# An expert stage on one core: two row tiles to a turn, half-height down matmuls, silus later, rows turned earlier, gathers in other chunks

## What is computed

```python
xn = _layernorm(x, axis=-1)
s = _L0_attn_ref(xn, w_qkv, w_out)
g = _silu(_L0_ffn_ref(xn, gate_w, wg, wu, wd))
x = x + s * g
```

```python
expert_idx = jnp.argmax(logits, axis=-1)
g = jnp.einsum('th,ehd->etd', xf, wg)
u = jnp.einsum('th,ehd->etd', xf, wu)
inter = jnp.square(jax.nn.relu(g)) * u
out = jnp.einsum('etd,edh->th', inter * onehot.T[:, :, None], wd)
```

## Time and profile before

| | |
|---|---|
| median of 3 runs | 1468.5 us (1468.19, 1468.5, 1473.36) |
| the profiled execution | 1476.87 us |
| its span, first to last instruction | 1475.1 us |
| mean granted share of the TensorE clock | 0.995 |
| PE, DVE, ACT, POOL busy | 1447.4, 1342.1, 1193.1, 161.7 us |

### The profile page before, as it was taken

How to read it: one execution, slowest core, us unless ns; L and a number is a source line. 1 busy time by engine, 2 the same in 40 slices (tenths; PEclk the granted TensorE clock), 3 DMA queues, 4 the chain that set the end, 5 groups by cost and what they waited for, 6 DMA issues and landing times.

```text
span 1475.1 us, 32004 instructions
## 1 busy us (share of the span) xinstructions
PE 1447.4 (98%) x11201; PEld 650.2 (44%) x11201; DVE 1342.1 (91%) x1979; ACT 1193.1 (81%) x2381; POOL 161.7 (11%) x221
## 2 busy tenths in 40 slices
PE   7999999999999999999999999999999999999988
PEld 5655444443485443444444444444444444444326
DVE  6689999999846998999999999999999999999806
ACT  3653488889867997898888898888898988998990
POOL 5333322200001221000000000000010000000110
PEclk9999999999999998999999999999999999999999
DMA  5875244426254455323233353332323523333323
GB/s 181 275 203 149 60 85 84 77 46 120 44 180 101 80 109 101 48 45 46 40 48 47 47 104 48 48 48 44 45 46 47 101 44 46 48 48 48 70 70 118
DMA packets 79801, 119.55 MB, mean 81 GB/s; under 512 B 28962, under 2 KB 66210, under 8 KB 72738
## 3 DMA queue, kind: packets, MB, share of 16 engines
q1 hardware_dynamic: 73714, 105.82, 36.2%
q0 software_dynamic: 3072, 8.39, 2.4%
q10 hardware_dynamic: 2896, 3.62, 0.7%
HBM read 77.15 MB, written 39.71 MB: 79 GB/s over the span
## 4 chain that ended last, share of the span: by engine, by line
PE 86%; DMA 8%; ACT 2%; issue 2%; DVE 1%; SPq 0%; POOL 0%; POOLq 0%; ACTq 0%
PE ps L1244 35%; PE ps L1258 33%; DMA gate<-ys_d,arena 7%; PE ps L1232 5%; PE ps L1160 3%; ACT arena L659 2%; PE ps L1438 2%; PE ps L1161 1%; PE ps L1391 1%; PE ps L1375 1%; PE ps L1193 1%; PE ps L1185 1%; PE ps L1172 1%; PE ps L1342 1%; PE ps L1137 0%
## 5 line engine op out<-in xcount | busy, mean ns | idle before, releaser
L1232 PE MATMUL ps<-ks,qs 48*128 48x512 f32 x1984 | 689.1, 443 | 0.0
L1244 PE MATMUL ps<-qs,ks 50*128 50x512 f32 x2048 | 679.2, 435 | 0.5 <-ACT arena L663 0.3
L810 DVE TENSOR_REDUCE arena<-ps 128x1 f32<-128x512 f32 x992 | 635.7, 676 | 12.4 <-PE ps L1232 12.2
L659 ACT ACTIVATE arena<-ps 128x512 f32<-128x512 f32 x1056 | 566.8, 606 | 78.8 <-PE ps L1244 67.0
L813 DVE TENSOR_REDUCE arena<-ps 128x1 f32<-128x1024 f32 x496 | 601.1, 1212 | 2.3 <-PE ps L1232 2.2
L659 ACT ACTIVATE x_sb<-ps 128x512 f32<-128x512 f32 x992 | 535.4, 598 | 64.1 <-PE ps L1244 47.9
L1244 PEld LDWEIGHTS ps<-qs,ks 50*128 50x128 f32 x2048 | 327.7, 185 | 475.6 <-issue 179.9
L1232 PEld LDWEIGHTS ps<-ks,qs 48*128 48x128 f32 x1984 | 325.0, 184 | 11.2 <-issue 3.0
L1258 PE MATMUL ps<-arena 128*32 128x256 f32 (+1 forms) x3104 | 308.6, 469 | 9.3 <-ACT arena L659 4.1
L1258 PE MATMUL ps<-x_sb,arena 128*32 128x256 f32 (+1 forms) x2960 | 291.1, 465 | 0.0
L1258 PEld LDWEIGHTS ps<-arena 128*32 128x32 f32 x3104 | 62.4, 108 | 129.1 <-issue 125.3
(11 more groups left out here) (116 smaller groups left out, 623.6 us busy)
## 6 DMA issues: line engine op xcount, KB each, us to landing
qs<-parts_d SPq DMA_DIRECT2D x186, 128.0 KB
ks<-parts_d SPq DMA_DIRECT2D x186, 128.0 KB
parts_d<-arena SPq DMA_DIRECT2D x64, 256.0 KB, 2.8
xs_d<-arena SPq DMA_DIRECT2D x13, 384.0 KB, 3.6
arena<-xs_d SPq DMA_DIRECT2D x13, 384.0 KB, 4.0
ys_d<-arena SPq DMA_DIRECT2D x13, 384.0 KB, 2.8
x_sb<-in_x SPq DMA_DIRECT2D x2, 2048.0 KB, 13.2
onum_d<-arena SPq DMA_DIRECT2D x124, 32.0 KB
```

The lines of the kernel that those rows point to most:

```text
L659: nc.scalar.activation(prob_of(pi, s, kb)[:, c * W:(c + 1) * W], ps[:, bank, :], ACT.Exp, scale=SCALE).then_inc(exp_done[bank], 1)
L810: nc.vector.tensor_reduce(most[head_slot][:, tile, u:u + 1], ps[:, AB + lo, :], AX.X, ALU.max).then_inc(a_reduced[u], 1)
L1232: ins = nc.tensor.matmul(ps[:, AB + c, :], qs[head_slot][ABASE:ABASE + KR, tile * P:(tile + 1) * P].bitcast(F32R), ks[head_slot][ABASE:ABA ...
L1244: nc.tensor.matmul(ps[:, bank, :], ks[s][at:at + KS, kb * P:(kb + 1) * P].bitcast(F32R), qs[s][at:at + KS, c * W:(c + 1) * W].bitcast(F32R ...
```

## The change

Two tiles, 2j and 2j+1, share a step j of PE, ACT and DVE. Each tile's hidden rows fill half of a 128-column `inter`, so one transpose serves both, and one tile's hidden rows come out on partitions 0 to 63, the other's on 64 to 127. The down weights are loaded twice, to both partition halves; each down matmul contracts 64 rows. For odd tiles POOL first copies the expert's lower-half weights to one of two buffers (`stage_down`), for even ones PE reads them by register. Rows are turned two tiles ahead, into banks 0 and 5 in turn, and `xsT` has four buffers. ACT takes the silus of tiles 2j-6 and 2j-5 at the head of its step j. `hr`, `hu` and the new weight buffers take the place of `turn`, which is no longer needed then. POOL's two memsets for zeroed halves go. SC is 11.

```diff
-    TB, EB, YB = 0, 1, 6
+    TBS, EB, YB = (0, 5), 1, 6
+    XB = 4
     XR = 3
-    SC = 14
+    SC = 11
...
-                for i in range(2):
-                    sp.dma_start(wd2[0:DE, :, :].rearrange("p (c i) d -> p c i d", i=2)[:, :, i, :],
-                                 wd_in[i * DE:(i + 1) * DE, :, :]).then_inc(expert_weights, 16)
+                for half in range(2):
+                    for i in range(2):
+                        rows = wd2[half * DE:(half + 1) * DE, :, :].rearrange("p (c i) d -> p c i d", i=2)
+                        sp.dma_start(rows[:, :, i, :], wd_in[i * DE:(i + 1) * DE, :, :]).then_inc(expert_weights, 16)
 
...
                 act.wait_ge(xs_turned, i + 1)
-                if i >= 2:
-                    act.wait_ge(hid_done, i - 1)
-                nc.scalar.copy(xsT[i % 2], ps[:, TB, 0:D].rearrange("p (k t) -> p k t", k=KC)).then_inc(xs_out, 1)
+                if i >= XB:
+                    act.wait_ge(hid_done, i - XB + 1)
+                nc.scalar.copy(xsT[i % XB], ps[:, TBS[i % 2], 0:D].rearrange("p (k t) -> p k t", k=KC)).then_inc(xs_out, 1)
 
...
-                for i in range(NF + 2):
-                    if i + 1 < NF:
-                        turned_out(i + 1)
-                    if i < NF:
-                        act.wait_ge(hid_done, i + 1)
-                        if i >= 2:
-                            act.wait_ge(inter_ready, i - 1)
-                        nc.scalar.activation(hr[i % 2], ps[:, EB + i % 2, 0:DE], ACT.Relu).then_inc(relu_done, 1)
-                    if i >= 2:
-                        act.wait_ge(y_done, i - 1)
-                        g, z = divmod(i - 2, FG)
-                        if g >= XR and z == 0:
-                            act.wait_ge(y_stored[g % XR], g // XR * 16)
-                        nc.scalar.activation(ysb[g % XR][:, z, :], ps[:, YB + i % 2, 0:D], ACT.Silu).then_inc(y_out, 1)
+                turned_out(1)
+                for j in range(NF2 + 3):
+                    for i in (2 * j - 6, 2 * j - 5):
+                        if 0 <= i < NF:
+                            act.wait_ge(y_done, i + 1)
+                            g, z = divmod(i, FG)
+                            if g >= XR and z == 0:
+                                act.wait_ge(y_stored[g % XR], g // XR * 16)
+                            nc.scalar.activation(ysb[g % XR][:, z, :], ps[:, YB + i % 2, 0:D], ACT.Silu).then_inc(y_out, 1)
+                    for i in (2 * j, 2 * j + 1):
+                        if i + 2 < NF:
+                            turned_out(i + 2)
+                        if i < NF:
+                            act.wait_ge(hid_done, i + 1)
+                            if i >= 2:
+                                act.wait_ge(inter_ready, i - 1)
+                            nc.scalar.activation(hr[i % 2], ps[:, EB + i % 2, 0:DE], ACT.Relu).then_inc(relu_done, 1)
 
...
-                for i in range(NF + 1):
-                    if i < NF:
+                for j in range(NF2 + 1):
+                    for i in (2 * j, 2 * j + 1):
+                        if i >= NF:
+                            continue
                         dve.wait_ge(relu_done, i + 1)
                         nc.vector.tensor_tensor(hu[i % 2], hr[i % 2], ps[:, EB + i % 2, DE:2 * DE], ALU.mult).then_inc(hu_ready, 1)
                         dve.wait_ge(hu_ready, i + 1)
-                        if i == 0:
-                            dve.wait_ge(pads_zeroed, 3)
-                        if i >= 2:
-                            dve.wait_ge(inter_turned, i - 1)
-                        nc.vector.tensor_tensor(inter[i % 2][:, 0:DE], hu[i % 2], hr[i % 2],
+                        if j >= 2:
+                            dve.wait_ge(inter_turned, j - 1)
+                        nc.vector.tensor_tensor(inter[j % 2][:, i % 2 * DE:(i % 2 + 1) * DE], hu[i % 2], hr[i % 2],
                                                 ALU.mult).then_inc(inter_ready, 1)
-                    if i >= 1:
-                        dve.wait_ge(inter_turned, i)
-                        if i >= 3:
-                            dve.wait_ge(y_done, i - 2)
-                        nc.vector.tensor_copy(interT[(i - 1) % 2], ps[:, PVB, 0:P]).then_inc(inter_out, 1)
+                    if j >= 1:
+                        dve.wait_ge(inter_turned, j)
+                        if j >= 3:
+                            dve.wait_ge(y_done, 2 * (j - 2))
+                        nc.vector.tensor_copy(interT[(j - 1) % 2], ps[:, PVB, 0:P]).then_inc(inter_out, 1)
 
...
+            def stage_down():
+
+                pool.wait_ge(expert_ready, 1)
+                pool.wait_ge(expert_weights, 16 * 8)
+                pool.wait_ge(v_staged[1], FB + 1)
+                for i in range(1, NF, 2):
+                    g, z = divmod(i, FP)
+                    if z == 1:
+                        packed = pool.value_load(expert[0:1, g:g + 1], min_val=0, max_val=E ** FP - 1)
+                    which = pool.snap(packed // E ** z % E, min_val=0, max_val=E - 1)
+                    if i >= 4:
+                        pool.wait_ge(y_done, i - 3)
+                    if i > 1:
+                        pool.wait_ge(down_staged, i // 2)
+                    nc.gpsimd.tensor_copy(down_up[i // 2 % 2][DE:P, :].unsqueeze(1),
+                                          wd2[DE:P, bass.ds(which, 1), :]).then_inc(down_staged, 1)
+
...
-            nc.gpsimd.memset(wd2[DE:P, :, :], 0.0).then_inc(pads_zeroed, 1)
-            pool.wait_ge(pads_zeroed, 2)
-            for i in range(2):
-                ins = nc.gpsimd.memset(inter[i][:, DE:P], 0.0)
-            ins.then_inc(pads_zeroed, 1)
-            pool.wait_ge(pads_zeroed, 3)
             for pi in range(2, FB):
                 for s in range(2):
                     stage(0, pi, s, pi)
             for s in range(2):
                 stage(0, FB, s, FB)
+            stage_down()
             collect(0, SC)
...
-                if i:
-                    pe.wait_ge(xs_out, i)
+                if i >= 2:
+                    pe.wait_ge(xs_out, i - 1)
                 for k in range(KC):
-                    last = nc.tensor.transpose(ps[:, TB, k * P:(k + 1) * P], xs[g % XR][:, z, k * P:(k + 1) * P], ident[:])
+                    last = nc.tensor.transpose(ps[:, TBS[i % 2], k * P:(k + 1) * P], xs[g % XR][:, z, k * P:(k + 1) * P], ident[:])
                 last.then_inc(xs_turned, 1)
 
...
             def experts():
...
+                pe.wait_ge(a_reduced[GROUP_OF[TBS[1] - AB]], past(FB * 2 * KB + AHEAD - KB))
+                turn_sorted(1)
+                pe.wait_ge(expert_weights, 16 * 8)
+                for j in range(NF2 + 2):
+                    for i in (2 * j, 2 * j + 1):
+                        if i + 2 < NF:
+                            turn_sorted(i + 2)
+                        if i < NF:
+                            pe.wait_ge(xs_out, i + 1)
+                            if i >= 2:
+                                pe.wait_ge(relu_done, i - 1)
+                                pe.wait_ge(hu_ready, i - 1)
+                            for k in range(KC):
+                                last = nc.tensor.matmul(ps[:, EB + i % 2, 0:2 * DE], xsT[i % XB][:, k, :],
+                                                        wgu[:, k, bass.ds(which[i], 1), :], start=(k == 0), stop=(k == KC - 1))
+                            last.then_inc(hid_done, 1)
+                        if i + 1 < NF:
+                            expert_of(i + 1)
+                    if 1 <= j <= NF2:
+                        if j == 1:
                             pe.wait_ge(o_out[1], past(FB))
+                        pe.wait_ge(inter_ready, min(2 * j, NF))
+                        if j >= 2:
+                            pe.wait_ge(inter_out, j - 1)
+                        nc.tensor.transpose(ps[:, PVB, 0:P], inter[(j - 1) % 2], ident[:]).then_inc(inter_turned, 1)
+                    if j >= 2:
+                        if j == 2:
                             pe.wait_ge(a_reduced[GROUP_OF[YB - AB]], past(FB * 2 * KB + AHEAD - KB))
+                        else:
+                            pe.wait_ge(y_out, 2 * (j - 2))
+                        pe.wait_ge(inter_out, j - 1)
+                        for i in (2 * j - 4, 2 * j - 3):
+                            if i >= NF:
+                                continue
+                            if i % 2:
+                                pe.wait_ge(down_staged, i // 2 + 1)
+                                rows, weights = slice(DE, P), down_up[i // 2 % 2][DE:P, :]
+                            else:
+                                rows, weights = slice(0, DE), wd2[0:DE, bass.ds(which[i], 1), :]
+                            which.pop(i)
+                            nc.tensor.matmul(ps[:, YB + i % 2, 0:D], interT[j % 2][rows, :], weights,
+                                             start=True, stop=True).then_inc(y_done, 1)
+                pe.wait_ge(inter_out, NF2)
```

(20 more changed lines are left out.)

## The result

The changed kernel took 1485.73 us in the median of five runs (1482.12 to 1488.15), against 1468.5 for five of the kernel before (1468.19 to 1473.36). The ratio is 1.0092, with a 95% interval from 1.0068 to 1.0116: slower by 0.9%.

What follows compares the result with a forecast made beforehand. PE was taken to bound the kernel, busy 98% of the span. From a base of 1468.5, -9.6 for the stage and +11.7 for waits gave +2.1: 1470.6 us; range 1466 to 1476, with two rivals 1462 to 1479.

Steps and rivals of the forecast that it cites:

- The pair step: Expert stage: PE's passes 1.43, down matmuls 0.44, switches 0.40, so 2.27 us, 2.31 with register loads, against 2.80 before.
- the two switches together: PE's changes between full and half height around the down matmuls lose 0.2 us each, 0.40 a pair.
- Rival (d): The down matmuls' halves don't run side by side, or only in part: +3.2 or +6.2, 1473.8 or 1476.8; chance 0.08.
- its lower form: The four half-height down-matmul passes take three slots instead of two: +3.2 us, 1473.8.
- The saving: Expert stage without waits for rows: 19.5 pairs at 2.31 instead of 2.80 us, -9.6 us.
- Emptying the stage: End of the expert stage, taken as equal; the last down matmul's wait for two silus is at most +0.8 us.
- The gate on the loads: SP's row loads, held behind stores and later silus, make PE wait five times 2.34 us before row transposes: +11.7 us.
- The clock: PE's granted clock in the expert stage stays up through the waits of 2.34 us; nothing added to the sum.
- rival (c): The clock falls in the five expert-stage waits of 2.34 us, giving 11 us more: 1481.6; chance 0.12.
- The profile and the median: A staging-copy stall behind the experts costs the profiled execution 7.95 us; most runs lack it, the one at 1473.36 holds part.
- Rival (a): The median run does hold the 7.95 us staging-copy stall, which the smaller chunks remove: 1462.6; chance 0.17.
- Costs taken as nothing: POOL's 19 weight copies, removed memsets, two more weight loads on SP's queue and PE's wait for bank 5: no time.

Runs made afterwards that it cites:

- the first experiment: The changed kernel with SP's row loads issued one group earlier, ahead of a store whose silu they had waited for: 1460.2 us, ratio 0.9926.
- second experiment: The kernel before with only the scatters and gathers cut at 11 and 22 tiles instead of 14 and 28: 1470.14 us in 12 runs, ratio 0.9991.

## Why the prediction was wrong

- **The pair step** was right: 2.27 without register loads, 2.22 measured; half-height passes side by side, and 2.22 - 1.43 - 0.44 = 0.35 for the two switches together. The gap at 408.16 is priced like those of the earlier trace rows. The Trainium skill's rule that changing the tiling mode drains the engine (TensorEngine Tiling (Array Packing), Key Properties) agrees with it. Rival (d) is out, its lower form too, since both second passes start together.
- **The saving** of the stage without waits came out right, 9.6 forecast and 9.1 by the intervals of the first experiment, but in part by luck. The row transposes gained more, 53.2 - 41.9 = 11.3, since a pair of tiles took 2.2 on average and not 2.31. Emptying the stage, which the sum took as equal but for 0.8, gave 2.2 back (49.5 against 47.3 from the last row transpose to the copy).
- **The gate on the loads** was right in place, number and size: five waits of 2.34 forecast, five with 12.1 in all in the trace, and no others. Taking the gate away and moving it by one pair both showed it.
- **The clock** is the step that failed. The forecast let PE's waits of 2.34 us leave the clock up, from one wait of 1.36 that did and one of 3.53 that didn't, so the sum had nothing for it; rival (c) had it with a chance of 0.12 and 11 us, 1481.6. What the runs showed: a fall with four of the five waits, worth 5.5 us in the stage, and none there once the waits were filled. Another 7.4 us went behind the last row transpose, with the clock down there too; the sum had nothing for that either, and its cause stays open. Together, -9.1 + 12.1 + 5.5 + 7.4 = +15.9, against +2.1 forecast and 15.95 measured between the copies. So (c) had the right mechanism for the stage and a price too high for it (2.2 a fall, where 5.5 in four are 1.4), and its total comes near by the second stretch, which it did not have. The range left most of (c) out and ended 6.7 us below the measured time. The rows excluded neither end, and the one of 1.36 carried more than it could: here the same wait of the last head is followed by a fall:

```profile
1420.66 1.94 PE L1278 MATMUL ps<-arena 128*32 128x512 f32 x8 [1.36 <-issue]
```

The window behind that wait:

```profile
1420.60:1423.80 3.20, 3.14 (x16) 0.86 (x20) 0.25 (x1) 0.85 (x2) 0.00 (x0) 0.50 0.18 42
```

- **The profile and the median.** That the median doesn't hold the stall was right (second experiment). That the run at 1473 would hold part of it is not borne out: with the chunks cut smaller such runs remain. Rival (a) is out. The base of 1468.5, from three runs, was itself 2 to 3 us low by the later runs (1471.79 and 1470.65); that moves the forecast to some 1473 and does not save it.
- **Costs taken as nothing**: POOL's weight copies took 0.40 each, and PE's waits name none of them.

## What to carry to other kernels

When a consumer is moved later, look for what another queue holds behind it: SP's in-order list tied a load to a store, and a store released two steps later put a transfer of 3.8 us on PE's path; issuing the load ahead of the store removed it. A wait of PE of two microseconds can have a second price, the clock behind it: in the stage four falls cost 5.5 us beside the 12.1 of the waits, and filling the waits with matmuls kept the clock up. Where the rows lie on both sides of such a wait, take the fall as a likely case and let the range hold it. And before all of a loss is put down to one cause, see where it lies: 7.4 us of this one lay behind the stage, where filled waits didn't remove it in every run.

## What was not expected

The length of a wait does not settle whether the clock falls behind it: 2.50 us at 432.43 was not followed by a fall and 2.36 at 411.28 was, and 1.36 in the last head was not in the kernel before and was in the changed one. Just behind the expert stage the clock falls in some executions of the old and of the new order alike (with the chunks alone, with nine fills, with loads ahead and chunks of 14); no run aimed at it, and what sets it off there stays open.
